# Preparations reordered: modulation products first, W_Q and W_K split in two parts, gates at the end of pair 0

## The reference

```
mod = (silu(c) @ wmod).reshape(16, 6, 1, 128)
sa, ca, ga, sb, cb, gb = (mod[:, j] for j in range(6))
ga = (2 * (ga >= 0) - 1) * maximum(abs(ga), 0.25)      # gb likewise
h = layernorm(x) * (1 + ca) + sa
q, k, v = h @ W_Q, h @ W_K, h @ W_V                    # per head
probs = softmax(where(causal_mask, -1e6, q k^T / sqrt(64)))
x = x + ga * (concat_heads(probs v) @ W_out + b_out)
h = layernorm(x) * (1 + cb) + sb
x = x + gb * moe_top2(h, W1, b1, W2, b2, Wr, br)
```

## Time and profile before

| | us |
|---|---|
| median of 3 runs | 2023.12 (2021.97 to 2023.38) |
| the profiled execution | 2025.12 |
| its span, first to last instruction | 2023.3 |
| PE busy | 1979.4 (98%) |
| DVE busy | 1694.6 (84%) |
| ACT busy | 1582.1 (78%) |
| POOL busy | 737.8 (36%) |

### The profile page before, as it was taken

The page is one execution under the profiler, slowest core; times in us unless marked ns, Lnnn a source line. Parts: engine busy times, 40 slices in busy tenths (PEclk is TensorE's granted clock), DMA queues, the critical chain, the costliest instruction groups (busy, mean ns, idle before and its releaser), DMA issues. The chain is left out here.

```text
span 2023.3 us, 46361 instructions
## 1 busy us (share of the span) xinstructions
PE 1979.4 (98%) x12703; PEld 1543.2 (76%) x12703; DVE 1694.6 (84%) x4518; ACT 1582.1 (78%) x3765; POOL 737.8 (36%) x1214
## 2 busy tenths in 40 slices
PE   6999999999999999999999998799999999999998
PEld 5777777777777777777777776578888888888886
DVE  6887888888888887888888876799999999999997
ACT  5888888888888888888888886677777777777775
POOL 3444444444444444444444444122222222222222
PEclk9999999999999999999999999899999999999999
DMA  4000000000000000000000000311121111111120
GB/s 128 7 2 0 0 0 0 0 0 0 0 0 0 0 0 0 0 0 0 0 0 0 0 1 1 125 48 47 54 75 54 47 47 52 47 47 47 48 75 24
DMA packets 42252, 49.46 MB, mean 24 GB/s; under 512 B 3112, under 2 KB 24160, under 8 KB 42208
## 3 DMA queue, kind: packets, MB, share of 16 engines
q1 hardware_dynamic: 41952, 48.41, 7.5%
q0 software_dynamic: 256, 0.53, 0.1%
HBM read 44.47 MB, written 4.46 MB: 24 GB/s over the span
## 5 line engine op out<-in xcount | busy, mean ns | idle before, releaser
L285 POOL TENSOR_SCALAR probs<-probs,rdenom 128x512 f32<-128x512 f32 (+3 forms) x1024 | 524.8, 538 | 699.0 <-DVE rdenom L690 699.0
L542 ACT ACTIVATE probs<-probs,neg_max 128x256 f32<-128x256 f32 (+3 forms) x1024 | 567.9, 555 | 72.9 <-DVE neg_max L681 70.8
L681 DVE CUSTOM_DVE_ANT_0 probs<-banks,mask_w 128x256 f32<-128x256 f32 (+3 forms) x1024 | 435.0, 481 | 84.4 <-PE banks L347 82.9
L1060 ACT ACTIVATE hidden<-banks,b_cols 128x512 f32<-128x512 f32 x512 | 348.8, 686 | 194.6 <-PE banks L926 191.7
L1176 DVE TENSOR_TENSOR hid_lo<-hidden,hid_hi 128x512 fp32r<-128x512 f32 x512 | 379.4, 751 | 52.5 <-ACT hid_hi L1068 39.4
L373 PE MATMUL banks<-ident,probs 128*128 128x128 f32 x2560 | 340.6, 276 | 3.3 <-POOL probs L285 2.3
L674 DVE COPY probs_T<-banks 128x512 f32<-128x512 f32 x384 | 258.4, 687 | 91.1 <-PE banks L373 91.0
L1000 POOL TENSOR_TENSOR acc<-acc,y_w 128x512 f32<-128x512 f32 x112 | 159.5, 1424 | 467.7 <-DVE y_w L1189 467.7
L373 PEld LDWEIGHTS banks<-ident,probs 128*128 128x128 f32 x2560 | 288.9, 141 | 49.2 <-DVE neg_max L681 19.2
L388 PE MATMUL banks<-probs_T,v_sb 128*64 128x512 f32 (+3 forms) x2048 | 303.9, 439 | 1.6 <-DVE probs_T L674 1.6
L388 PEld LDWEIGHTS banks<-probs_T,v_sb 128*64 128x64 f32 x2048 | 135.5, 136 | 148.5 <-issue 119.0
(11 more groups left out here) (140 smaller groups left out, 3377.2 us busy)
## 6 DMA issues: line engine op xcount, KB each, us to landing
w_rows<-w_kept SPq DMA_DIRECT2D x128, 256.0 KB, 3.9
x_all<-in_L_attn_resid_dram SPq DMA_DIRECT2D x16, 256.0 KB, 2.6
out_dram<-y_result SPq DMA_DIRECT2D x16, 256.0 KB, 2.4
w_raw<-in_L_ffn_W_dram SPq DMA_DIRECT2D x12, 256.0 KB, 5.1
hidden<-in_L_ffn_W_dram SPq DMA_DIRECT2D x4, 256.0 KB, 6.2
v_sb<-in_L_attn_W_Q_dram SPq DMA_DIRECT2D x1, 512.0 KB, 5.7
v_sb<-in_L_attn_W_K_dram SPq DMA_DIRECT2D x1, 512.0 KB, 6.5
v_sb<-in_L_attn_W_V_dram SPq DMA_DIRECT2D x1, 512.0 KB, 7.8
```

Of the source, the lines that this page charges most:

```text
L285: pool.tensor_scalar(part, part, rdenom[:, p % 2, 4 * h + r:4 * h + r + 1], 1.0, ALU.mult, ALU.mult)\
L542: act.activation(part, part, ACT.Exp, bias=neg_max[:, p % 2, col:col + 1], scale=-1.0, accum_out=denom[:, p % 2, col:col + 1]).then_inc(p_ ...
L681: dve.tensor_tensor_reduce(out=probs[:, p % 2, h, at:at + n], in0=S_BANK[u][h][:, col:col + n], in1=mask_w[:, 512 - n:512], scale=-SCALE, ...
L1060: act.activation(hidden[:, e % 2, c, :], banks[:, c, :], ACT.Gelu, bias=b1_cols[:, e * HC + c:e * HC + c + 1]).then_inc(hid, 1)
```

## The change

- PE: the six products of the modulation stand ahead of h_transposes(0), and the transposes of the biases, with their wait for load_b, ahead of the projections for pair 0.
- DVE: the rest of silu stands ahead of ln_stats(0). The copies of the biases, with their wait for b_ps, stand ahead of rest_h(0).
- W_Q and W_K are rounded and split in two parts: the first 128 columns, which pair 0 needs (round_first, split_first, with the semaphores first_rounded and first_split), and the other 896. PE waits for first_split ahead of pair 0's projections and for w_split 1 and 2 ahead of pair 1's.
- ACT: W_V is rounded within pair 0, behind the fourth exponential step, no longer ahead of pair 0.
- DVE: gates() moves from behind split_weights(2) to behind split_weights(3), the end of pair 0.

```diff
@@ PE, pair 0 @@
+                            if begin:
+                                pe.wait_ge(w_split, 1)
                             if has_next:
                                 project_q(*nxt)
+                            if begin:
+                                pe.wait_ge(w_split, 2)
                             if has_next:
                                 project_k(*nxt)
@@ PE, preparations @@
-                    h_transposes(0)
                     pe.wait_ge(silu_ok, 1)
                     pe.wait_ge(load_mod, 16)
                     for j in range(6):
                         mm = pe.matmul(s_banks[0][:, j * B:(j + 1) * B], wmod_sb[:, j * D:(j + 1) * D], silu_c,
                                        start=True, stop=True)
                     mm.then_inc(mod_ps, 1)
-                    pe.wait_ge(w_split, 1)
-                    project_q(0, 0)
-                    pe.wait_ge(w_split, 2)
-                    project_k(0, 0)
+                    h_transposes(0)
                     pe.wait_ge(load_b, 32)
                     pe.transpose(g_bank[:, B:B + E * HC], b1_rows, ident[0:E * HC, 0:E * HC])
                     pe.transpose(g_bank[:, 64:64 + E], b2_rows, ident[0:E, 0:E]).then_inc(b_ps, 1)
+                    pe.wait_ge(first_split, 1)
+                    project_q(0, 0)
+                    pe.wait_ge(first_split, 2)
+                    project_k(0, 0)
@@ ACT @@
                     def round_weights(i):
+                        begin = P if i < 2 else 0
-                        act.activation(hi, raw, ACT.Copy).then_inc(w_rounded, 1)
+                        act.activation(hi[:, begin:QK], raw[:, begin:QK], ACT.Copy).then_inc(w_rounded, 1)
+
+                    def round_first(i):
+
+                        (hi, lo), raw = flat_w[i], raw_w[i]
+                        act.wait_ge(load_w[i], 16)
+                        act.activation(hi[:, 0:P], raw[:, 0:P], ACT.Copy).then_inc(first_rounded, 1)
...
-                    round_weights(0)
+                    round_first(0)
                     act.wait_ge(mod_ok, 1)
                     h_evac(0)
                     round_h(0)
-                    round_weights(1)
+                    round_first(1)
+                    round_weights(0)
                     round_q(0, 0, False)
                     round_k(0, 0)
-                    round_weights(2)
+                    round_weights(1)
...
                             exponentials(b, p, 1, 0)
+                            if begin:
+                                round_weights(2)
                             exponentials(b, p, 0, 1, [2])
@@ DVE, preparations @@
-                    ln_stats(0)
                     dve.wait_ge(exp_c, 1)
                     link(dve.tensor_scalar(e1_c, e_c, 1.0, None, ALU.add))
                     link(dve.reciprocal(sig_c, e1_c))
                     dve.wait_ge(c_ok, 1)
                     dve.tensor_tensor(silu_c, c_cols, sig_c, ALU.mult).then_inc(silu_ok, 1)
+                    ln_stats(0)
                     ln_apply(0)
+                    split_first(0)
                     dve.wait_ge(mod_ps, 1)
...
-                    split_weights(0)
-                    rest_h(0)
-                    split_weights(1)
-                    rest_q(0, 0)
-                    rest_k(0, 0)
                     dve.wait_ge(b_ps, 1)
                     dve.tensor_copy(b1_cols[:, :], g_bank[:, B:B + E * HC])
                     dve.tensor_copy(b2_cols[:, :], g_bank[:, 64:64 + E]).then_inc(b_ok, 1)
+                    rest_h(0)
+                    split_first(1)
+                    split_weights(0)
+                    rest_q(0, 0)
+                    rest_k(0, 0)
+                    split_weights(1)
@@ DVE, pair 0 @@
                             if begin:
                                 split_weights(2)
-                                gates()
...
                             if begin:
                                 split_weights(3)
+                                gates()
```

More of the change, by code:

```diff
@@ L186, in adaln_moe_kernel @@
             w_split = sem("w_split")
+            first_rounded = sem("first_rounded")
+            first_split = sem("first_split")
             qk_ps = sem("qk_ps")
@@ L728, in split_weights, with split_first @@
                         (hi, lo), raw = flat_w[i], (raw_w + [raw_wo])[i]
+                        begin = P if i < 2 else 0
                         dve.wait_ge(w_rounded, i + 1)
-                        dve.tensor_tensor(lo, raw, hi.bitcast(F32), ALU.subtract).then_inc(w_split, 1)
+                        dve.tensor_tensor(lo[:, begin:QK], raw[:, begin:QK], hi[:, begin:QK].bitcast(F32), ALU.subtract)\
+                            .then_inc(w_split, 1)
+                    def split_first(i):
+                        (hi, lo), raw = flat_w[i], raw_w[i]
+                        dve.wait_ge(first_rounded, i + 1)
+                        dve.tensor_tensor(lo[:, 0:P], raw[:, 0:P], hi[:, 0:P].bitcast(F32), ALU.subtract)\
+                            .then_inc(first_split, 1)
                     def gates():
```

## The result

| | before | changed |
|---|---|---|
| median, us | 2023.22 (14 executions, 2021.97 to 2025.43) | 2027.43 (14 executions, 2026.1 to 2028.96) |
| ratio | | 1.002, 95% interval 1.0013 to 1.0028 |
| the profiled execution, us (span) | 2025.12 (2023.3) | 2026.16 (2024.4) |

The forecast was 2024.1 in a range of 2021.0 to 2026.8. The median lies above the range.

A forecast was written before the change was run, and what follows sets the result against it. The loop was taken as TensorE-bound and untouched, so the start of its unbroken run counts, set by pair 1's first DVE mask: 31.6 against 30.54, +1.0, clock 0. Median 2023.12 + 1.0 = 2024.1 us, range 2021.0 to 2026.8.

The forecast's parts named there:

- The step that was to decide: End of pair 0 on DVE: gates queue behind W_out's split, so pair 1's first mask comes 1.0 us later.
- The sum: Pair 1's first mask on DVE: W_out's rounding ends 27.9, split 1.15, gates 2.54, giving 31.6 against 30.54.
- Every lead on DVE and ACT: Preparations and pair 0: modulation 2.9 us earlier, 1.7 left after the bias wait; k_lo 3.6 earlier, ACT 1.5.
- the clock, "I take 0": TensorE's granted clock behind the gap ahead of pair 1's transposes: could cost or save 1.5 us, taken as 0.
- the difference of +1.0: Net delay of pair 1's first mask, 1.0 us, added to the earlier median 2023.12 to give 2024.1.
- the clearly slower rival: Long gap leaves TensorE at 1.2 GHz far into pairs 1 and 2: +4.1 us, 2027.3, chance 0.06.
- the landing of the bias loads: Small loads on SP behind W_V, awaited before pair 0's projections: land at 11.2, bounds 6.6 to 12.35.
- The rival with the late landing: Small bias loads land as late as x, at 12.35: another 1.15 us later, 2025.3, chance 0.14.

The follow-up runs named there:

- before_again: The kernel before, unchanged, traced a second time: 2022.43 us.
- before_filled: The kernel before with 9 unread matmuls of 128x512 ahead of pair 1's scores and 9 ahead of the transposes behind them: median 2023.1 us, ratio 0.9996.
- gap_filled: The changed kernel with 22 unread matmuls of 128x512 behind pair 1's scores only: median 2025.19 us, ratio to the kernel before 1.0009.
- after_again: The changed kernel, unchanged, traced a second time: 2026.61 us.
- after_filled: The changed kernel with 11 unread matmuls behind pair 1's projections and 29 behind pair 1's scores: median 2026.18 us, ratio 1.0013.
- gates_first: The changed kernel with gates() ahead of W_out's split instead of behind it, at the end of pair 0: median 2025.03 us, ratio to before 1.0007.
- bias_late: The changed kernel with the bias transposes back behind pair 0's projections and their copies between q_lo and k_lo: median 2025.73 us, ratio to before 1.0011.
- modulation_first_only: The kernel before with only silu's rest ahead of the statistics and the modulation's products ahead of the norm's transposes: median 2020.29 us, ratio 0.9988.
- bias_late_gates_first: The changed kernel with the biases late again and gates() ahead of W_out's split: median 2023.06 us, ratio to before 0.9999.

## Why the prediction was wrong

**Right, by the trace of the same kind.** The step that was to decide did: gates behind W_out's split, with DVE waiting ahead of it. The sum was 27.9 + 1.15 + 2.54 = 31.6 for the mask; 31.18 and 31.27 were measured, with W_out's split at 27.32 and 27.41 where I had 27.9. hf at 9.64 (9.3 forecast), h_lo at 12.20 (12.0), scores at 17.43 (17.2), the first mask at 18.44 (18.5), transposes at 34.37 (34.8). Every lead on DVE and ACT was there and ended in DVE's wait. But that the two profiled executions differ by 1.04, as the sum has it, is luck: the start was 0.64 later and not 1.0, the way was 0.74 longer by the clock that I took as 0, and behind the first block the changed kernel's execution was 0.35 shorter (2025.12 - 1264.57 against 2026.16 - 1265.96).

**Wrong: the clock, "I take 0", together with the base.** This is the step that failed. I carried the difference of +1.0, worked out from one execution, over to the median. But that execution of before had lost TensorE's full clock ahead of T (it fell at 30.6, during pair 1's scores), and most had not: I noted that it stood 2.0 us above the median and didn't ask why. 33 of 101 executions of before took 2024.5 us or more, where this trace stands; before_again, in the lowest group, kept 1.00, and the filler of before_filled emptied the upper group. The group near 2023.2 has no trace; that only its scores of pair 0 are slow is an inference. The changed kernel idles 7.0 us ahead of the transposes and lost the clock in both of its traces. The way then took 7.6 to 7.8 us instead of 5.1, and filling the gap gives back 2.2 us in the median (gap_filled): that is the size of the term I took as 0. I had listed this mechanism as the clearly slower rival with 0.06, but let it act only on low clock beyond 3.7 us, which presumes that before pays those 3.7 each time. That rival's number, 2027.3, was met by luck: in the changed kernel's traces the low stretch behind T lasted 5.4 and 5.7 us, not the 9.8 that it asks for.

**Wrong in size: the landing of the bias loads.** I took 11.2, and a wait that takes 1.2 us of the lead (2.9 less 1.7). Five traces have this order; the transposes of the biases, released by that load, started at 11.61 (after), 11.70 (after_again), 11.75 (after_filled), 12.57 (gates_first) and 12.71 (gap_filled). The rival with the late landing had 0.14. The row of W_V in the changed kernel's DMA issues (KB, us to landing):

```profile
v_sb<-in_L_attn_W_V_dram SPq DMA_DIRECT2D x1, 512.0 KB, 8.1
```

From its issue at 3.19 that makes 11.29. In the same order of traces W_V landed at 11.29, 10.79, 11.39, 12.19 and 12.19, and the transposes that wait for the small loads started 0.3 to 0.9 us behind it. The Trainium skill, page "DMA: Bandwidth & Descriptors", section "Queues, rings and completion order", says that each DMA engine takes up the descriptors of one ring in order. These traces agree with it. The wait costs 1.7 us in the median (bias_late).

**The account of the 4.2 us.** The clock: with the gap filled, the changed kernel is 2027.43 - 2025.19 = 2.2 us faster. In the kernel before, the filler takes 0.2 off the median (2023.3, that of the 101 executions of before beside all these runs, to 2023.1). This small number comes of the median, which lies in the two thirds below 2024.5; in the set beside before_filled, where 17 of 33 took that or more, the filler took off 1.4 (2024.5 to 2023.1). The rest is the 2.1 by which the two filled kernels still differ (2025.19 - 2023.1), and I put it down to the start. That 2.1 + 2.2 - 0.2 makes 4.1 is no check: these are differences of the same four medians. As an estimate, an execution at full clock takes T + 1989.7 us (2022.19 at T = 32.51, 2025.83 at 36.21, 2022.43 at 32.61, and in modulation_first_only 2019.22 at 29.49), so that the two filled medians stand for T = 33.4 and 35.5. T in the typical execution is not read from a trace: the unfilled pairs of traces differ in it by 0.64 and 1.86, and both traces of the changed kernel are in the lower half of its times.

**The sum of the parts**: modulation first alone -2.8; with the weights in parts, W_V's rounding in pair 0 and the gates ahead of W_out's split, 2.8 are lost again (bias_late_gates_first against modulation_first_only). In their traces T is 1.37 later (30.86 against 29.49) and the way 2.13 longer (7.27 against 5.14), so more than half of this is again the clock, which fell in a gap of 4.41 us. What of the 1.37 is W_V's rounding between the exponentials, 1.04 on ACT by my sum, and what the weights in parts, wasn't tried by itself and stays open. The gates' place adds 2.4 to 2.7 (gates_first; bias_late against bias_late_gates_first), the bias wait 1.7 to 2.0.

**The rule of the Trainium skill** that I weighed and left out of the sum, page "TensorE: Matmul & The Clock Gate", section "HAM oscillation", says that a TensorE which waits long enough between two bursts begins the next one at half clock. The runs bear it out for the long gap, which is paid twice: idle 7.00 us and then 0.50 granted in both traces of the changed kernel; full clock, and 5.14 us for the way, when the same gap is filled with useless matmuls. They don't bear it out for every gap: behind the 4.32 us of gates_first the transposes began at 1.00, and in the first trace of before the clock fell while TensorE was at work, behind gaps of 0.78 and 2.13 us.

## What to carry to other kernels

A lead gained early is worth what is left at the place where the bound engine begins its unbroken run. Follow each queue there, and put small chains into waits that already exist, not behind the last one. Before a sum is carried from one profiled execution to the median, explain the distance between the two: if the profiled one is off by more than the effect, its trace may show another course than the typical run. A small load issued behind large ones on a queue belongs late in the order of its consumers.

## What the runs showed that I had not expected

- One and the same program had its granted clock at 0.50 or at 1.00 from 31 to 37 us, and it idled longer in the trace that kept 1.00 (2.06 us ahead of T against 1.32). The cost is 1.7 us on the way behind it; slow scores in pair 0, at the same idle time ahead of pair 1's scores (2.13), go with another 1.1 (T at 33.73 and 32.61).
- Useless matmuls can pay: 22 of them in a gap of 7 us made the kernel 2.2 us faster (2027.43 to 2025.19). In a gap whose end others wait for they cost: in after_filled they held the value products from 24.48 to 25.91.
- Nine small steps on DVE (53.80 to 55.9 us) cost 1.7 us in pair 3, where DVE counts as 84% busy over the span, and nothing visible in the preparations.
